# Attention scores in two half-height tiles of TensorE instead of one full-height product

## What is computed

```python
x = x + tanh(g_xattn[0]) * attention(layernorm(x), ctx)      # x: 16x512x512, ctx: 16x77x512
x = x + tanh(g_ffn[0])   * feed_forward(layernorm(x))        # 512 -> 2048 -> 512, with a sine
# attention, 16 heads of 32:
q, k, v = x1 @ Wq.T + bq, x2 @ Wk.T + bk, x2 @ Wv.T + bv
scores = einsum('bhnd,bhmd->bhnm', q, k) / sqrt(32)          # n: 512 rows, m: 77 keys
o = einsum('bhnm,bhmd->bhnd', softmax(scores), v)
return o @ Wo.T + bo
```

## Time and profile before

| | |
|---|---|
| median of 3 runs | 2233.33 us (2232.54 to 2234.48) |
| the profiled execution | 2231.39 us, span of its instructions 2229.6 us |
| TensorE matmul busy | 2185.5 us, 98% of the span |
| TensorE weight loads busy | 1826.8 us, 82% |
| VectorE, ScalarE, GpSimd busy | 65%, 54%, 18% |
| mean granted clock of TensorE | 0.995 of 2.4 GHz |

### The profile page before, as it was taken

How to read it: one execution, slowest core, us unless ns; L and a number is a source line. 1 busy time by engine, 2 the same in 40 slices (tenths; PEclk the granted TensorE clock), 3 DMA queues, 4 the chain that set the end, 5 groups by cost and what they waited for, 6 DMA issues and landing times.

```text
span 2229.6 us, 33283 instructions
## 1 busy us (share of the span) xinstructions
PE 2185.5 (98%) x10385; PEld 1826.8 (82%) x10385; DVE 1445.7 (65%) x2596; ACT 1213.6 (54%) x3571; POOL 408.0 (18%) x341
## 2 busy tenths in 40 slices
PE   8989999999999989999999999999999999999999
PEld 6778888888888877888888888888888888888887
DVE  5566776677767747766666566566566666665654
ACT  3477777777767745544454454444544544444444
POOL 5133333333333321101001011011011010110110
PEclk9999999999999999999999999999999999999999
DMA  7513232322232344223123122121231231231210
GB/s 231 180 33 99 79 84 79 102 80 76 86 95 86 84 133 123 67 57 76 57 56 75 56 38 74 51 62 62 51 75 56 56 75 56 56 71 58 40 38 20
DMA packets 269170, 169.38 MB, mean 76 GB/s; under 512 B 190928, under 2 KB 205788, under 8 KB 269066
## 3 DMA queue, kind: packets, MB, share of 16 engines
q1 hardware_dynamic: 267290, 167.63, 27.7%
q0 software_dynamic: 1344, 0.64, 0.2%
q10 hardware_dynamic: 432, 0.04, 0.0%
HBM read 108.86 MB, written 59.38 MB: 75 GB/s over the span
## 4 chain that ended last, share of the span: by engine, by line
PE 61%; DVE 1%; ACT 1%; issue 0%; ACTq 0%
PE m_bank L56 31%; PE pair_bank L56 31%; DVE w_split L1346 0%; DVE hidden L1379 0%; DVE turns L1375 0%; ACT relu L1306 0%; ACT hidden L1315 0%; ACT turns L1317 0%; DVE sine L1372 0%; DVE stats L173 0%; DVE relu L1362 0%; DVE x_in L198 0%; ACT sine L1322 0%; ACT L1322 0%; ACT w_split L1302 0%
## 5 line engine op out<-in xcount | busy, mean ns | idle before, releaser
L56 PE MATMUL m_bank<-xT,w_split 128*128 128x512 f32 x3072 | 740.2, 390 | 4.0 <-DVE w_split L1346 4.0
L56 PE MATMUL pair_bank<-w_split,relu 128*128 128x512 f32 x3072 | 738.4, 389 | 3.4 <-DVE relu L1362 3.2
L56 PEld LDWEIGHTS m_bank<-xT,w_split 128*128 128x128 f32 x3072 | 578.2, 188 | 124.7 <-DVE w_split L1346 4.4
L56 PEld LDWEIGHTS pair_bank<-w_split,relu 128*128 128x128 f32 x3072 | 576.2, 188 | 125.3 <-issue 3.6
L1322 ACT ACTIVATE sine<-turns 128x512 f32<-128x512 f32 x256 | 161.8, 632 | 392.2 <-DVE turns L1375 392.2
L998 ACT ACTIVATE exps<-pair_bank,exp_bias 128x77 f32<-128x77 f32 x1024 | 319.3, 365 | 65.7 <-DVE exp_bias L1044 65.5
L1306 ACT ACTIVATE relu<-hidden 128x512 fp32r<-128x512 f32 x256 | 161.8, 632 | 331.1 <-PE m_bank L56 231.1
L1362 DVE SCALAR_TENSOR_TENSOR relu<-hidden,relu 128x512 fp32r<-128x512 f32 x256 | 181.7, 710 | 201.0 <-ACT relu L1306 201.0
L1379 DVE SCALAR_TENSOR_TENSOR hidden<-sine,sine_gain,hidden 128x512 f32<-128x512 f32 x256 | 197.2, 770 | 169.9 <-ACT sine L1322 169.9
L193 POOL TENSOR_TENSOR rstd<-var_eps,minus_half 128x4 f32<-128x4 f32 x32 | 38.3, 1197 | 1191.1 <-DVE var_eps L189 1191.1
L998 ACT ACTIVATION_READ_ACCUMULATOR exps<-pair_bank,exp_bias 128x1 f32 x1024 | 252.0, 246 | 0.0
(11 more groups left out here) (117 smaller groups left out, 1931.3 us busy)
## 6 DMA issues: line engine op xcount, KB each, us to landing
x_in<-in_x_dram SPq DMA_DIRECT2D x16, 1024.0 KB, 5.6
residual<-in_x_dram SPq DMA_DIRECT2D x64, 256.0 KB, 2.6
x_scratch<-residual SPq DMA_DIRECT2D x64, 256.0 KB, 2.1
x_in<-x_scratch SPq DMA_DIRECT2D x16, 1024.0 KB, 5.6
residual<-x_scratch SPq DMA_DIRECT2D x64, 256.0 KB, 3.2
out_dram<-residual SPq DMA_DIRECT2D x64, 256.0 KB, 2.1
quad_scratch<-x_in SPq DMA_DIRECT2D x60, 256.0 KB, 5.2
x_in<-quad_scratch SPq DMA_DIRECT2D x60, 256.0 KB, 4.6
```

The costliest lines, as they stand in the source:

```text
L56: mm = pe.matmul(out, stationary(s), moving(m), start=first and n == 0, stop=last and n == len(PASSES) - 1)
```

## The change

The scores of a group come from two products over 64 rows of the array instead of one over 128. `k_diag` keeps two heads a row block: rows 0 to 63 hold heads 0 and 1 as a block diagonal of 64x154, rows 64 to 127 heads 2 and 3, in the same 154 columns. For each tile of query rows and each pass, first the upper 64 rows of `qT` and `k_diag` are multiplied, into bank 0 of `pair_bank[half]`, then the lower 64 rows, into bank 1. What was split over the banks by query tile is now split by head pair. `scores_view`, the index of the bias and of the input of the exponentials follow; `exps` and everything after it keep their layout.

```diff
+    ROW_TILES = 2
+    ROW_HEADS = HG // ROW_TILES
+    KEY_ROWS = P // ROW_TILES
-        k_diag = sb(att, "k_diag", [P, G, 2, GC], F32R)
+        k_diag = sb(att, "k_diag", [P, G, 2, ROW_HEADS * M], F32R)
         def load_keys(queue, b, g, loaded):
-                queue.dma_start(k_diag[rows, g, :, j * M:(j + 1) * M].bitcast(F32), k_parts[b, g, rows])\
+                queue.dma_start(k_diag[rows, g, :, j % ROW_HEADS * M:(j % ROW_HEADS + 1) * M].bitcast(F32), k_parts[b, g, rows])\
             def scores_view(half):
-                return pair_bank[half][:, :, 0:GC].rearrange("p n (h m) -> p n h m", m=M)
+                return pair_bank[half][:, :, 0:HALF * ROW_HEADS * M].rearrange("p r (u m) -> p r u m", m=M)
                     for n in range(HALF):
                         tile = HALF * half + n
-                        mm = matmul3(pe, pair_bank[half][:, n, 0:GC],
-                                     lambda p: qT[g % 2][p][:, tile * P:(tile + 1) * P],
-                                     lambda p: k_diag[:, g, p, :], True, True)
+                        for i, (s, m) in enumerate(PASSES):
+                            for r in range(ROW_TILES):
+                                rows = slice(KEY_ROWS * r, KEY_ROWS * (r + 1))
+                                mm = pe.matmul(pair_bank[half][:, r, n * ROW_HEADS * M:(n + 1) * ROW_HEADS * M],
+                                               qT[g % 2][s][rows, tile * P:(tile + 1) * P], k_diag[rows, g, m, :],
+                                               start=i == 0, stop=i == len(PASSES) - 1)
                     mm.then_inc(scores_full, 1)
                     for i in range(UR):
                         n, h = i // HG, i % HG
-                        e = act.activation(exps[half][:, n, h * M:(h + 1) * M], pair_bank[half][:, n, h * M:(h + 1) * M],
-                                           ACT.Exp, bias=exp_bias[half][:, i:i + 1], scale=SCALE,
+                        r, u = h // ROW_HEADS, n * ROW_HEADS + h % ROW_HEADS
+                        at = r * HALF * ROW_HEADS + u
+                        e = act.activation(exps[half][:, n, h * M:(h + 1) * M], pair_bank[half][:, r, u * M:(u + 1) * M],
+                                           ACT.Exp, bias=exp_bias[half][:, at:at + 1], scale=SCALE,
                                            accum_out=exp_sum[half][:, i:i + 1])
-                    dve.tensor_reduce(peak[half][:, :].rearrange("p (n h) -> p n h", h=HG), scores_view(half),
+                    dve.tensor_reduce(peak[half][:, :].rearrange("p (r u) -> p r u", r=ROW_TILES), scores_view(half),
                                       AX_X, ALU.max).then_inc(peak_ready, 1)
```

## The result

The changed kernel takes 2235.52 us (median of 20 runs, 2234.12 to 2241.48), the kernel before in as many runs beside it 2232.47 us. The ratio is 1.0020, 95% interval 1.0014 to 1.0026: slower by 0.2%, 3 us. The forecast was no difference, 2233 us, with 2225 to 2245 for its case and 2204 to 2325 with the rivals. So the time lies inside both ranges, but there is a difference, clear of the noise, where none was forecast.

What follows compares the result with a forecast made beforehand. TensorE was taken to bound the kernel. Load-bound score pairs plus drains came to 1.82 us a head group, 0.01 more than before, under 1 us over 64; everything else at nothing. Forecast 2233 us, likeliest case 2225 to 2245, range 2204 to 2325.

Steps and rivals of the forecast that it cites:

- Bound: Attention stage: TensorE sets the time, busy for 40.00 of 40 us.
- Both ways: Attention stage: a microsecond added to or taken from TensorE's work is one in the time.
- Load: Scores: a weight load of 64 rows takes 0.11 us, as for 128, and is not hidden behind 154 columns.
- p: Scores: distance from one pair of tile matmuls to the next, taken as 0.115 us, between 0.110 and 0.124.
- Drains: Around the scores: each change of tile height drains the array for 0.09 us; entering the lower tile costs 0.20 us.
- Case A: Scores: the two tiles overlap fully; 1.82 us a head group, 0.01 more than before; 2225 to 2245 us, chance 0.46.
- everything else of the change, at nothing: Outside the scores' distances: extra instructions, memset, key DMAs, maximum and exponentials add no time and no wait.
- case E: TensorE's clock: idle columns in the drains make it fall, in every fourth group or each; 2260 to 2335 us, chance 0.05.
- B: Scores: the two tiles' loads don't run side by side; plus 81 us, 2315, or 2322 with p = 0.115; chance 0.27.
- C: Scores: the loads overlap, the matmuls don't, 24 at 0.073 us; 2260 us, chance 0.07.
- D: Scores: each alternation of row block drains the array; some 326 us more, 2560 us, chance 0.05.
- Slower: Sign of the whole kernel's change: a time above what can be told from no change, about 4.5 us; chance 0.54.

Runs made afterwards that it cites:

- u4: The changed kernel with the loops over tiles and passes exchanged, three passes of the upper rows, then three of the lower: 2234.68 us, ratio 1.0011 to the kernel before.
- w1: The changed kernel with the third chunk's transposes between the two halves of the scores instead of behind them: 2268.72 us, ratio 1.0168 to the kernel before.
- w2: The kernel before with the third chunk's transposes between the two halves of the scores: 2251.74 us, ratio 1.0087 to the kernel before.
- r3: The kernel before, full height, with 154 instead of 308 moving columns in each score matmul: 2226.56 us against 2230.94, ratio 0.9985.
- s2: The changed kernel with 64 unused bytes a partition behind `k_diag`: 2236.72 us against 2232.53 for the kernel before, ratio 1.0018.

## Why the prediction was wrong, point by point

**Bound.** TensorE bound, right for the sign it was used for. "Both ways" was wrong: a saving of 20 us gave 4.4.

**Load.** 0.11 us for 64 rows as for 128, and load-bound behind 154 columns: shown, by full-height matmuls 0.11 apart and by tiles with 76 columns that are no closer than with 154. It is the figure of these fp32r loads: the first two loads of the transposes behind a drained array, 128 columns too, are 0.06 us apart.

**p.** Taken 0.115, measured 0.112 (11 p + 0.27 = 1.50 us). The upper bound of 0.124 rested on program order between the tiles; u4 showed that there is none here.

**Drains.** 0.20 us in, measured 0.17; with the way out 0.24 to 0.31 by the ledger, 0.24 by w1 against w2, 0.30 by r3. The Trainium skill, "TensorEngine Tiling (Array Packing)", section Key Properties, says that a switch of mode drains and that tiles run in parallel. Both hold here: 0.17 us of idle 58 times, and pairs of loads that start together.

**Case A's sum.** It had 0.01 us more a head group; with the old addresses the trace gives 0.02 less (0.07 a batch). So case A came in as the mechanism and, to 0.03 us a group, in size: 1 to 2 us over the program.

**The step that failed** is "everything else of the change, at nothing". The prediction went through the memset, the DMAs and the readers of the scores, and stopped there. A tensor that shrinks by 4928 bytes moves v_diag, exps, probs, probsT, oT and some small tensors, and one product of each head group became 0.04 us longer, 64 x 0.04 = 2.6 us. That term belonged into A's sum. With the tiles' own gain of 1.2 us (0.02 a group) it makes the 1.4 us of the batch distances.

**The second part of it** is case E. It was treated as a rival, with a chance of 0.05 and at least 26 us, as if the clock either fell in every fourth group or not at all. What happened lies between. Counted in us of full clock, what was not granted adds up to 10 in the trace before (a mean of 0.995) and to 12 and 19 in the two traces of the change (0.995 and 0.992); the added part is in the first two batches and at the loop's heads, where TensorE waited anyway. It goes with 1.6 us in the median and 5 to 7 us in single runs. The row for it was in the prediction, the wait of 2.01 us with the clock behind it. But the length of the wait doesn't decide alone. At the next two loop heads of the same trace TensorE waited longer, and the clock stayed up, 1.00 over the 6 us from 538 and from 627:

```profile
538.22 0.66 PE L898 MATMUL t_bank<-ident,probs 128*128 128x128 f32 x4 [2.17 <-DVE probsT L1034]
626.93 0.66 PE L898 MATMUL t_bank<-ident,probs 128*128 128x128 f32 x4 [2.10 <-DVE probsT L1034]
```

**Chances.** Slower had 0.54, same 0.24. That the time moved to the slower side is luck as far as this sum goes: 0.44 of the 0.54 were B, C, D and E, a loss of 26 us or more, and none of them came. The 3 us lie in what the prediction called the same, since it took 4.5 us for what can be told from no change; 20 executions of each kernel told 3.

## What stays open

How the 3 us split exactly. The medians have 1.6 us for the tiles of two batches (1.24 left of 2.8) and the rest for the addresses, but the intervals are as wide as these parts. Restoring the addresses alone (s1) took nothing off the median, with a clock of 0.993 or less in every run. Why that kernel's clock fell more often than the change's own isn't known, nor what makes it fall behind one wait and not behind a longer one.

## What to carry to other kernels

When products are split into tiles to halve the columns, ask first what a weight load costs: here 0.11 us a load capped the gain at 0.139 to 0.112 us a product, and changing the height twice, 0.24 to 0.31 us, ate the 0.28 that was left. A tensor made smaller moves all that is allocated behind it, so compare a product that was not touched, and give a pad back before judging the change. And where an engine is busy almost without a gap, look at the few waits that it has before counting a saving in full: here 20 us saved on TensorE were 4.4 in the time.

## What the runs showed of the hardware

- Instructions of two disjoint row tiles are not held in program order against each other: by the distances of u4, a load and matmul three pairs later started 10 ns after the first.
- Leaving and entering the 64-row tiles costs 0.24 to 0.31 us together, of which 0.17 is idle before the first load.
- 12 matmuls of 512 columns took 2.72, 2.75 or 2.79 us, by where the tensors behind `k_diag` lie; of the product's own operands only the stationary one had moved.
- The mean clock of a run was 0.994 to 0.997 before, 0.990 to 0.995 with tiles, 0.987 to 0.990 with tiles of 76 columns, 0.986 to 0.992 with full height and 154 columns, and 0.986 to 0.991 in w1, which takes nothing off but changes height more often. In the attention loop of all traces the falls lie behind TensorE's waits of 1.6 to 3.3 us; but waits of 2.1, 2.2 and (s2) 2.6 us had no fall.
